# Feed-forward of a decoder layer on one core: the sixteen gathers of the first expert rows issued with at most two under way, each summed as its own gather lands

## The reference, cut to what matters

```python
xf = _layernorm(x).reshape(-1, 512)             # 2048 tokens
probs = softmax(xf @ gate_w.T)                  # 8 experts
top_p, top_i = top_k(probs, 2)                  # two experts for each token
combine = zeros(n, 8).at[arange(n)[:, None], top_i].set(top_p)
h = silu(xf @ expert_fc1[e].T) * (xf @ expert_fc2[e].T)        # 352 wide, for each expert e
out_e = h @ expert_proj[e].T
y = einsum('ne,enc->nc', combine, out_e)
y = y + sigmoid(xf @ shared_gate_w.T) * shared(xf)             # a dense expert, 1408 wide
x = x + y
```

## Time and profile before

| | us |
|---|---|
| median of 3 runs (lowest, highest) | 1520.15 (1517.0, 1522.9) |
| the profiled execution, its own time | 1516.7 |
| its span, first to last instruction | 1514.9 |
| first gather into `early` issued | 1439.0 |
| last gather into `early` issued | 1457.9 |
| first gather into `late` issued | 1479.1 |
| last gather into `late` issued | 1503.5 |

### The profile page before, as it was taken

How to read it: one execution, slowest core, us unless ns; L and a number is a source line. 1 busy time by engine, 2 the same in 40 slices (tenths; PEclk the granted TensorE clock), 3 DMA queues, 4 the chain that set the end, 5 groups by cost and what they waited for, 6 DMA issues and landing times. The chain is left out here.

```text
span 1514.9 us, 24037 instructions
## 1 busy us (share of the span) xinstructions
PE 1340.9 (89%) x8442; PEld 1077.9 (71%) x8442; DVE 872.5 (58%) x1522; ACT 474.6 (31%) x739; POOL 511.0 (34%) x350
## 2 busy tenths in 40 slices
PE   5899999994699999999856999999999999999960
PEld 4677777773567777776445888888878799999950
DVE  5666666665587788787466665655574422222224
ACT  3222222233166665566612211111111133233210
POOL 1122222124543444332023035431160563664045
PEclk9999999997799999999968999999999999999985
DMA  8000000010555555455078013230000334343246
GB/s 326 1 1 1 0 0 0 0 56 35 167 176 159 167 146 158 147 146 151 24 280 334 2 57 117 77 136 21 22 35 14 141 134 143 136 171 109 65 138 228
DMA packets 92731, 159.83 MB, mean 106 GB/s; under 512 B 7920, under 2 KB 61296, under 8 KB 90352
## 3 DMA queue, kind: packets, MB, share of 16 engines
q1 hardware_dynamic: 86384, 124.19, 25.1%
q0 software_dynamic: 6272, 34.61, 6.4%
HBM read 88.77 MB, written 69.47 MB: 104 GB/s over the span
## 5 line engine op out<-in xcount | busy, mean ns | idle before, releaser
L1583 DVE SCALAR_TENSOR_TENSOR residual<-c_yp,c_shared,residual 128x512 f32<-128x512 f32 x176 | 127.4, 745 | 143.4 <-PE c_yp L43 142.9
L1014 DVE TENSOR_REDUCE b_mx<-b_rt 128x4 f32<-128x1024 f32 x128 | 156.4, 1222 | 52.3 <-PE b_rt L853 52.2
L1133 ACT ACTIVATE b_pf<-b_rt,b_zero 128x1024 f32<-128x1024 f32 x128 | 142.9, 1116 | 121.0 <-PE b_rt L865 120.8
L41 PE MATMUL c_fc<-c_xh,c_w 128*128 128x512 f32 x352 | 137.1, 390 | 0.0
L43 PE MATMUL c_fc<-c_xh,c_w 128*128 128x512 f32 x352 | 137.0, 389 | 0.0
L42 PE MATMUL c_fc<-c_xl,c_w 128*128 128x512 f32 x352 | 137.0, 389 | 0.0
L41 PE MATMUL c_fc<-c_ring,c_xTl 128*128 x312 | 105.5, 338 | 2.6 <-DVE c_xTl L1588 2.6
L1597 DVE TENSOR_TENSOR c_hTl<-c_eh,c_hTh 128x384 fp32r<-128x384 f32 x39 | 21.8, 558 | 146.0 <-ACT c_hTh L1707 133.6
L1683 ACT ACTIVATE c_s<-c_fc 128x512 f32<-128x512 f32 x44 | 26.3, 598 | 240.0 <-PE c_fc L43 234.5
L42 PE MATMUL c_fc<-c_ring,c_xTh 128*128 x312 | 101.1, 324 | 0.0
L43 PE MATMUL c_fc<-c_ring,c_xTh 128*128 x312 | 101.0, 324 | 0.0
(11 more groups left out here) (297 smaller groups left out, 3446.1 us busy)
## 6 DMA issues: line engine op xcount, KB each, us to landing
weights_b<-b_pack SPq DMA_DIRECT2D x128, 200.0 KB
c_eraw<-in_c_we POOLq DMA_DIRECT2D x8, 2176.0 KB, 9.6
b_pack<-b_hi SPq DMA_DIRECT2D x64, 256.0 KB, 2.5
c_xe<-c_rows_in SPq DMA_DIRECT2D x39, 256.0 KB, 2.9
c_rows_out<-c_ye SPq DMA_DIRECT2D x39, 256.0 KB, 2.0
c_rows_in<-c_xe SPq DMA_DIRECT2D x19, 512.0 KB
c_rows_out<-c_xe SPq DMA_DIRECT2D x19, 512.0 KB
c_wraw<-in_c_ws SPq DMA_DIRECT2D x11, 768.0 KB, 4.3
```

What stands on the lines that cost most here:

```text
L41: nc.tensor.matmul(out, ll, rh, start=start, stop=False)
L1014: nc.vector.tensor_reduce(out=mx[:, :, 2 * p:2 * p + 2].rearrange("p t e -> p e t"), in_=rt[:, 0:2, :].rearrange("p e (t s) -> p e t s", s ...
L1133: nc.scalar.activation(pf[:, s:s + 2, :], rt[:, 2:4, :], ACT.Exp, scale=XD ** -0.5, bias=zero[:, :]).then_inc(e_done, 1)
L1583: nc.vector.scalar_tensor_tensor(out=X[:, t, :], in0=yp[:, (n * 4 + k) % 3, :], scalar=shared[:, t:t + 1], in1=X[:, t, :], op0=ALU.mult, o ...
```

## The change

Two semaphores take the place of one for the gathers into `early`: those of even tiles count on one, those of odd tiles on the other. GpSimd waits before gather t (from t = 2 on) until gather t - 2 has landed, so at most two are under way. On DVE the sum of tile t waits for gather t alone, where all sums waited for all sixteen. The order of instructions on every engine stays; the gathers into `late` and their sums are as before.

```diff
-        landed0, landed1 = sem("landed0"), [sem("landed1%d" % g) for g in range(G)]
+        landed0, landed1 = [sem("landed00"), sem("landed01")], [sem("landed1%d" % g) for g in range(G)]
...
             def gather(t, k, into):
                 nc.gpsimd.indirect_dma_start(
                     out=into[:, t, :], out_offset=None, in_=rows_out,
-                    in_offset=bass.IndirectOffsetOnAxis(ap=rows[:, k, t:t + 1], axis=0)).then_inc(landed1[t // 4] if k else landed0, 16)
+                    in_offset=bass.IndirectOffsetOnAxis(ap=rows[:, k, t:t + 1], axis=0)).then_inc(landed1[t // 4] if k else landed0[t % 2], 16)
...
             for t in range(NT):
+                if t >= 2:
+                    pool.wait_ge(landed0[t % 2], 16 * (t // 2))
                 gather(t, 0, early)
...
                     else:
-                        dve.wait_ge(landed0, 16 * NT)
+                        dve.wait_ge(landed0[t % 2], 16 * (t // 2 + 1))
```

## The result

The changed kernel takes 1508.88 us (median of 5 runs, 1504.37 to 1510.0), the kernel before beside it 1517.0 (5 runs, 1515.42 to 1522.9): ratio 0.9934, 95% interval 0.9908 to 0.996, so 6 to 14 us faster. That is the forecast's direction and cause, at a little over half of its size (14.9 us). The profiled execution takes 1510.0, its span is 1508.2.

A forecast was written before the change was run, and what follows sets the result against it. TensorE, busy 89%, bounds most of the kernel; near the end a hole does. Hole 14.1 us less cap 3.8, plus held gather 4.8, less collisions 0.2: 14.9 off 1520.15, put at 1505 us; range 1500 to 1523.

The forecast's parts named there:

- The hole: Last slots' ye copies: TensorE's signals reach ACT late, costing 14.1 us; forecast that the cap removes it, chance 0.42.
- Rivals A: Hole lasts while early gathers are under way, however many; capped gathers end 10 us later: 1530 us, or 1525; chance 0.14.
- B: Hole in the slot loop equally long in both kernels, gain 0, 1520 us; chance 0.37 together with Rival C.
- D: Hole in the slot loop shrinks to a third or half: 5 to 9 us gained, 1511 to 1515; chance 0.07.
- Rival C: Hole only in the profiled execution, made by recording: 2.6 us gained, 1517.5, or 3.8 lost; chance 0.37 together with B.
- The pace: Capped early gathers on GpSimd: 3.9 us a pair (3.5 to 4.1), GpSimd free at 1468.8, costing 3.8 of 14.1 us.
- The collision with the sums: Gathers 12 to 15 and late's first meet DVE's sums: up to 2.5 us on GpSimd's queue, 0.2 taken.
- The 5.72 us row before: First late gather on GpSimd, read as kept out by early's sums; its 4.8 us loss was forecast to go.
- The tail: From the second late gather to the end: 29.8 us, forecast unchanged by the edit.

The follow-up runs named there:

- before_again: The kernel before, unchanged, timed again with a new profile: 1516.75 us, ratio to before 0.9997.
- after_again: The changed kernel, unchanged, timed again with a new profile: 1506.23 us, ratio to before 0.9925.
- second group: Runs on one chip, among them both kernels unchanged once more; the kernel before took 1518.06 us there (23 runs).
- own_sems: Against the changed kernel: no cap, 16 semaphores, each sum of early behind its own gather; 1503.6 us, ratio to before 1.0032.
- cap3: The changed kernel with at most three gathers of early under way instead of two: 1504.24 us, ratio to before 1.0037.
- cap2_wait_all: The changed kernel with its cap of two, but the sums of early behind all sixteen landings: 1505.35 us, ratio to before 1.0048.
- cap3_again: The changed kernel with three gathers under way instead of two, timed a second time on another chip: ratio to before 1.0033.
- cap3_split: Against the changed kernel: three gathers under way, and sums of early and late interleaved in groups; ratio to before 1.001.
- paced: own_sems with a GpSimd memset behind each gather of early, spacing them 1.74 us on average without waits for landings: ratio to before 1.0048.

## Why the prediction came out as it did

**The hole, right.** The step that carried the forecast, that at most two gathers under way let TensorE's signals through, held in both traces of the changed kernel (22.6 us to the last copy where the estimate was 23.0), against 37.1 and 37.8 before. Rivals A (hole longer), B (as long) and D (shorter) are out for the cap of two. A cap of three left 1.8 us of it in one trace, D's kind of outcome, with less left than D's third or half. Whether the number under way, the pace or the wait for a landing does it is not shown, since the cap changes all three.

**Rival C, against the evidence.** By C the timed runs should have gained 2.6 us; they gained 8.1 and 11.8. And the same program takes 1517 to 1518 us where its traces have the hole, 1498 where its relatives' have none. But C pointed at what I had left out: that the same program may or may not have the hole. I took one execution's stall for a property of the kernel.

**The pace, right.** 3.85 us a pair against 3.9.

**The collision with the sums, mis-sized.** I took 0.2 us for gathers of early that meet running sums, on the ground that waits for landings absorb most, with 0.51 each as the bound. It was one gather held for 4.64 us, 3.7 over its own time, and nothing absorbed it: gather 14 was issued right behind, gather 15 only when 13 had landed, at 32.1 instead of 28.6 us after the first. The second late gather was then issued at 35.1 instead of the forecast 31.3 us after the first. The 5.72 us row before showed the same price for one gather; I should have charged it as something that can recur wherever a run of sums meets an issue, and not as gone with its place.

**The tail, assumed equal.** From the second late gather to the end it was 1508.2 - 1477.27 = 30.9 us instead of 1514.9 - 1485.17 = 29.7 (29.8 in the prediction, which started the stretch at 1485.1): 1.2 us lost. This is not the edit's doing as far as shown: the same stretch is 28.9 us in before_again and 29.6 in after_again, so it differs by about 1 us between traces of one kernel.

Together: 14.9 forecast, less 3.8, less 1.2, is the 9.9 that the traces show. In the second group the traces show 75.7 - 64.8 = 10.9. The medians show 8.1 and, in the second group, 11.8 (1518.06 - 1506.23). That 1508.88 us came within 3.9 of the 1505 is in part luck: the kernel before took 1517.0 beside it and not the 1520.15 from which the prediction subtracts; the gain itself was 6.8 us short.

**Where the hole is absent** the changed kernel was not timed. Its relatives there are 0.3 to 0.5% slower than before (own_sems, cap3 twice, cap2_wait_all), so I expect the same of it; that is an expectation, not shown. Why even own_sems, without a cap, is 4.6 us slower there than before stays open: there is no trace of before on such a chip. A guess from the rows: before, the sums start at the last landing, 22.1 us after the first gather instead of 19.9 in own_sems, and the first late gather may then hit a seam and not be held, which would be worth 5.70 - 0.95 = 4.75 us. The 18 to 19 us between the two bands would then be the hole's 14.1 and this.

**What makes the hole** stays open as well. Shown is: signals of TensorE arrive up to 13 us late (xTh at 1461.93 for transposes over at 1448.9) while its instructions start on time up to these transposes, and ScalarE's signals to VectorE arrive promptly (hTl at 1455.94, right after hTh at 1455.43). As the profile models where matmuls end, it can't tell a late signal from work that was itself held up at its end. On two of the four chips of the groups it comes with gathers issued every 1.26 us, and not with two under way; the load on the DMA engines alone doesn't make it, nor do semaphores. What differs between the chips, or the sessions, no run here could tell.

## What to carry to other kernels

A stall with no releaser that the trace can name is worth a second profile on another chip before a change is sized by it. When two engines can keep each other out, charge the worst row wherever their runs can meet, and remove the meeting rather than the place: a memset that makes the step of the sums 10 ns longer gave back 4 us here, another order of them 6 to 8 us. A limit on transfers under way costs its pace at once, so it should be no tighter than the stall needs: three under way with the sums split gained more than two under way where before has the hole (ratio 0.9898 against 0.9925 and 0.9934) and cost nothing measurable elsewhere (1.001). How much of that is the cap and how much the order of the sums was not taken apart where the hole is; where the hole is absent, the order is worth 2.9 us (cap3_again to cap3_split).

## What the runs showed of the hardware that was not expected

- One program, four chips, two times: 1498 to 1499 and 1517 to 1518 us. The difference goes with a stall of TensorE's signals that in the slower band comes in each of the four traces without a cap, at the same place (copies of ye 18.1 to 18.2 us apart), and is absent in the two traces without one in the faster band (own_sems, paced). The kernel before itself was not traced there.
- Back-to-back VectorE sums with two SBUF inputs keep a GpSimd gather out for as long as they run (5.70 us in own_sems, ending 0.82 us after them) or let it in at every second seam (1.02 us each, 1.32 to 1.33 apart, in cap2_wait_all).
